# Turning h and the rows of x on VectorE, one block deeper, in a mixture-of-experts loop

## The reference

```python
x = hidden_states.reshape(-1, H)
logits = x @ gate_w
mult, sel = _sparse_mixer_routing(logits)
w = jnp.sum(mult[:, :, None] * (sel[:, :, None] == jnp.arange(E)[None, None, :]), axis=1)
h = jax.nn.silu(jnp.einsum('th,ehf->etf', x, w1)) * jnp.einsum('th,ehf->etf', x, w3)
out = jnp.einsum('etf,efh,te->th', h, w2, w)
```

## Time and profile before

| | |
|---|---|
| runs of the kernel before | 699.46, 698.66 and 1225.76 us; median 699.46 |
| profiled execution, first to last instruction | 697.2 us |
| busy in it: PE / DVE / ACT / POOL | 612.1 / 404.9 / 239.2 / 283.3 us |
| expert loop, from block 1's up to the last up | 327.36 to 663.45 us |
| end of the loop to the end of the span | 663.45 to 697.2 us |

### The profile page before, as it was taken

One profiled execution on the slowest core, in us unless ns is written; L12 is line 12 of the kernel. 1 busy time (PEld: TensorE's weight loads), 2 busy tenths in 40 slices (PEclk: granted clock), 3 DMA queues, 4 the chain that ended last, 5 costly groups with the idle time before them and its releaser, 6 DMA issues.

```text
span 697.2 us, 13581 instructions
## 1 busy us (share of the span) xinstructions
PE 612.1 (88%) x3780; PEld 482.2 (69%) x3781; DVE 404.9 (58%) x1214; ACT 239.2 (34%) x471; POOL 283.3 (41%) x198
## 2 busy tenths in 40 slices
PE   6999899798798875388999999999999999999940
PEld 2444469586366654367888888888888888888830
DVE  2566588766748879876544545445454454544524
ACT  3555540002876551224223242232422323321204
POOL 7000020012364456566516738167381373751112
...
GB/s 277 328 335 336 126 1 243 1 1 177 5 2 1 32 168 120 113 99 57 169 68 30 105 121 30 211 30 115 111 43 198 30 30 196 30 30 32 31 21 235
DMA packets 54003, 74.78 MB, mean 107 GB/s; under 512 B 13392, under 2 KB 50640, under 8 KB 52688
## 3 DMA queue, kind: packets, MB, share of 16 engines
...
...
## 4 chain that ended last, share of the span: by engine, by line
PE 68%; DVE 14%; POOL 5%; ACT 5%; DMA 4%; issue 3%; POOLq 0%; DVEq 0%; SPq 0%; ACTq 0%
PE bank L2197 26%; PE bank L2217 12%; PE bank L1769 7%; PE bank L1928 4%; PE bank L2207 4%; POOL experts_w L817 3%; DVE region L1259 2%; DVE region L1257 2%; DMA region<-slots 1%; PE bank L1819 1%; PE bank L1778 1%; PE bank L2152 1%; DVE small L1276 1%; PE bank L1785 1%; PE bank L2096 1%
## 5 line engine op out<-in xcount | busy, mean ns | idle before, releaser
L2197 PE MATMUL bank<-experts_w,experts_x 128*128 (+1 forms) x864 | 216.1, 399 | 3.6 <-POOL experts_w L817 2.3
L2197 PEld LDWEIGHTS bank<-experts_w,experts_x 128*128 128x128 f32 x864 | 157.0, 188 | 37.1 <-issue 4.4
L1701 DVE TENSOR_TENSOR region<-region,bank 128x512 f32<-128x512 f32 x72 | 49.5, 687 | 159.9 <-ACT region L1083 159.9
L1083 ACT ACTIVATE region<-bank 128x512 f32<-128x512 f32 x72 | 43.0, 597 | 238.5 <-PE bank L2197 238.5
L830 POOL DMA_INDIRECT total<-region,rid x36 | 55.8, 1549 | 165.2 <-DVE region L1715 105.8
L2217 PE MATMUL bank<-experts_w 128*128 (+1 forms) x864 | 120.9, 289 | 1.9 <-DVE experts_w L1705 1.9
L2217 PEld LDWEIGHTS bank<-experts_w 128*128 128x128 f32 x864 | 107.8, 191 | 2.2 <-issue 2.2
L817 POOL TENSOR_TENSOR experts_w<-wstage,experts_w 128x3072 f32 x12 | 83.6, 6964 | 0.5
L698 POOL TENSOR_TENSOR small<-small 128x4 f32<-128x4 f32 (+5 forms) x19 | 25.0, 1320 | 105.4 <-DVE small L1268 86.7
L1769 PE MATMUL bank<-xcol,region 128*128 128x512 f32 x128 | 59.0, 619 | 7.3 <-DMA xcol<-in_xT 5.7
L1155 DVE SCALAR_TENSOR_TENSOR region<-bank,convw,region 128x511 f32<-128x511 f32 (+2 forms) x48 | 35.9, 748 | 34.9 <-ACT region L873 33.0
...
...
## 6 DMA issues: line engine op xcount, KB each, us to landing
wstage<-in_w_exp SPq DMA_DIRECT2D x8, 3072.0 KB, 10.8
...
```

Source lines behind the costliest of these rows:

```text
L1083: act.activation(gsil[:, u], bank[2 * u][:, :], ACT.Silu).then_inc(sil_done, 1)
L1701: dve.tensor_tensor(hmid[:, u], gsil[:, u], bank[2 * u + 1][:, :], ALU.mult).then_inc(mid_done, 1)
L2197: mm = pe.matmul(bank[2 * u + m][:, :], (xTh, xTl)[a][:, s, k, :], moving(off, w, m * KD * F + k * F + u * HALF, HALF), start=(k == 0 and ...
```

## The change

- **Turns move from PE to DVE.** DVE's transpose turns blocks of 32x32. So h is first regrouped: `middle` writes `hmid` in four column groups, and SP's `regroup` copies each with a DMA from SBUF to SBUF into 32 partitions of `hgrp`, four DMAs a block of 128 pieces of 1 KB. DVE's `turn` (L1800) then turns 512 columns at once into the PSUM bank that PE wrote before. In the same way `load_rows` fetches x with four DMAs a block, in pieces of 32 values (128 B), and `rows` begins with a DVE transpose (L1720). The metadata gets its own small load, `load_meta`.
- **One block deeper.** In block g PE does up(g) and down(g-2). DVE does rows(g+1), row_meta(g-1), middle(g), turn(g-1), low_turned(g-1), weigh(g-2).
- **Weights in two parts.** SP loads the first 4096 columns (`load_up`) and the last 2048 (`load_down`) apart, in its own loop, behind the regrouping. ACT casts the first part (`high_up`), ahead of silu(g, 0). POOL takes its low part (`low_up`), and one block later splits the second part (`split_down`), behind a send.
- **The last block** is turned by PE (`last_turn`), into buffers of its own. `NB` grows from 42 to 48, so 8 pairs stand behind an `If` in place of 5 (two are taken). Each expert gets at least two blocks.

The diff, its core:

```diff
-NB = (2 * T + 2 * P + E * (P - 1)) // P + 1
-NB += NB % 2
+NB = 48
...
+        def rows_by_part(rows, a):
+            return rows[:, 0:D].rearrange("t (k a r) -> a t k r", a=NC, r=CH)[a]
...
+            def regroup(g, s):
+                if not isinstance(g, int) or g >= 2:
+                    sp.wait_ge(turned, 2 * g - 2)
+                    sp.sem_inc(sp_gate, 1)
+                sp.wait_ge(mid_done, 2 * g + 2)
+                for c in range(NC):
+                    sp.dma_start(hgrp[CH * c:CH * (c + 1), s].rearrange("p a q r -> p (a q r)"),
+                                 hmid[:, s, c].rearrange("p q r -> p (q r)")).then_inc(grouped[s], 16)
...
+            def load_ahead(g):
+                with sp.If(sp.value_load(tab_load[0:1, bass.ds(g - 1, 1)], min_val=0, max_val=1) > 0):
+                    event = event_of(g - 1)
+                    e = expert_of(event + 2)
+                    sp.wait_ge(w_low_up, event)
+                    load_up(e)
+                with sp.If(sp.value_load(tab_load[0:1, bass.ds(g - 2, 1)], min_val=0, max_val=1) > 0):
+                    event = event_of(g - 2)
+                    e = expert_of(event + 2)
+                    sp.wait_ge(w_ready, event + 2)
+                    load_down(e)
...
+            def pair(p):
+                regroup(2 * p - 1, 1)
+                load_ahead(2 * p - 1)
+                regroup(2 * p, 0)
+                load_ahead(2 * p)
...
+                    with pool.If(begins(g)):
+                        low_up(g)
+                    if isinstance(g, int) and g == 1:
+                        continue
+                    send_block(g - 2, s)
+                    with pool.If(begins(g - 1)):
+                        split_down(g - 1)
...
+            def load_rows(g, s):
+                rows = slots[bass.ds(slot_of(g), P), :]
+                act.wait_ge(xg_turned, g - 1)
+                for a in range(NC):
+                    act.dma_start(xq[CH * a:CH * (a + 1), s], rows_by_part(rows, a)).then_inc(xq_loaded[s], 16)
+
+            def load_meta(g, s):
+                slot = slot_of(g)
+                if not isinstance(g, int) or g >= 2:
+                    act.wait_ge(meta_done, g - 1)
+                act.dma_start(xm[:, s], slots[bass.ds(slot, P), D:ROW]).then_inc(xm_loaded[s], 16)
...
+            def high_up(g):
+                with act.If(act.value_load(tab_first[0:1, bass.ds(g, 1)], min_val=0, max_val=1) > 0):
+                    event = act.value_load(tab_event[0:1, bass.ds(g, 1)], min_val=1, max_val=E - 1)
+                    off = act.value_load(tab_noff[0:1, bass.ds(g, 1)], min_val=0, max_val=max(slot_at))
+                    act.wait_ge(up_done, 2 * g)
+                    act.wait_ge(w_up_loaded, 16 * event)
+                    act.sem_inc(act_gate, 1)
+                    act.copy(hi_of(off)[:, 0:ACT_PART], wstage[:, 0:ACT_PART]).then_inc(w_hi, 1)
...
+                    load_rows(g + 2, s)
+                    load_meta(g, s)
+                    if not start:
+                        high_up(g)
+                    silu(g, 0)
                     silu(g, 1)
-                    high_turned(g, 0)
-                    with act.If(act.value_load(tab_first[0:1, bass.ds(g, 1)], min_val=0, max_val=1) > 0):
-                        next_high(g)
-            def next_high(g):
-                event = act.value_load(tab_event[0:1, bass.ds(g, 1)], min_val=1, max_val=E - 1)
-                off = act.value_load(tab_noff[0:1, bass.ds(g, 1)], min_val=0, max_val=max(slot_at))
-                if not isinstance(g, int) or g:
-                    act.wait_ge(y_done, g)
-                act.wait_ge(w_loaded, 16 * event + 32)
-                act.sem_inc(act_gate, 1)
-                act.copy(hi_of(off)[:, 0:ACT_PART], wstage[:, 0:ACT_PART]).then_inc(w_hi, 1)
+                    for u in range(2):
+                        high_turned(g - 1, u)
+                    if start:
+                        high_up(g)
...
+                dve.wait_ge(xq_loaded[s], 32 * (g - s) + 64)
+                if isinstance(g, int) and g == 0:
+                    wait_drained(dve, ("f3", 1))
+                else:
+                    dve.wait_ge(xgT_done, g)
+                dve.transpose(bank[7][:, 0:D].rearrange("p (k r c) -> p c k r", k=KD, c=NC),
+                              xq[:, s].rearrange("p (c k r) -> p c k r", c=NC, k=KD)).then_inc(xg_turned, 1)
...
+            def middle(g, s, u):
                 dve.wait_ge(sil_done, 2 * g + (u + 1))
-                dve.tensor_tensor(hmid[:, u], gsil[:, u], bank[2 * u + 1][:, :], ALU.mult).then_inc(mid_done, 1)
-
-            def low_turned(g, u):
+                by_part = "p (c a r) -> p c a r"
+                dve.tensor_tensor(hmid[:, s, :, 4 * u:4 * u + 4].rearrange("p a c r -> p c a r"),
+                                  gsil[:, u].rearrange(by_part, a=NC, r=CH),
+                                  bank[2 * u + 1][:, :].rearrange(by_part, a=NC, r=CH), ALU.mult).then_inc(mid_done, 1)
+
+            def turn(g, s, u):
+                if u == 0:
+                    dve.wait_ge(grouped[s], 32 * (g - s) + 64)
+                if not isinstance(g, int) or g:
+                    dve.wait_ge(hTl_done, 2 * g + (u - 1))
+                dve.transpose(bank[4 + u][:, :].rearrange("p (c r a) -> p c a r", a=NC, r=CH),
+                              hgrp[:, s, :, 4 * u:4 * u + 4].rearrange("p a c r -> p c a r")).then_inc(turned, 1)
+
+            def low_turned(g, u, turned_in, high, low):
                 dve.wait_ge(hTh_done, 2 * g + (u + 1))
...
-                    row_meta(g + 1, 1 - s)
+                    row_meta(g - 1, 1 - s)
+                    for u in range(2):
+                        middle(g, s, u)
+                    for u in range(2):
+                        turn(g - 1, 1 - s, u)
+                    for u in range(2):
+                        low_turned(g - 1, u, bank[4 + u], hTh, hTl)
+                    if not isinstance(g, int) or g >= 2:
+                        weigh(g - 2, s)
...
+                    for u in range(2):
+                        up(g, s, u, off)
+                    if isinstance(g, int) and g == 1:
+                        continue
+                    off = offset_of(event_of(g - 2))
+                    for u in range(2):
+                        down(g - 2, u, off, hTh, hTl)
             pair(0)
+            pair(1)
             npair = pe.value_load(tab_n[0:1, 0:1], min_val=SURE, max_val=NB // 2)
-            with pe.Fori(0, SURE - 1) as it:
-                pair(it + 1)
+            with pe.Fori(0, SURE - 2) as it:
+                pair(it + 2)
             with pe.Fori(0, NB // 2 - SURE) as it:
                 with pe.If(npair - it > SURE):
                     pair(it + SURE)
...
+            off = offset_of(event_of(last - 1))
+            down(last - 1, 0, off, hTh, hTl)
+            for u in range(2):
+                last_turn(last, u)
+            down(last - 1, 1, off, hTh, hTl)
             off = offset_of(event_of(last))
-            turn(last, 1)
-            down(last, 0, off)
-            down(last, 1, off)
+            for u in range(2):
+                down(last, u, off, endTh, endTl)
```

266 lines of the change are left out of this document (133 added, 133 removed).

## The result

| | before | after |
|---|---|---|
| median of the runs | 700.64 us (4 runs) | 729.41 us (4 runs) |
| profiled execution | 697.2 us | 726.8 us |
| block 2's first silu to block 35's (33 blocks) | 319.0 us | 339.3 us |

One of the four executions of before took 1225.76 us and is left out of the ratio. The ratio after/before is 1.041 (95% interval 1.039 to 1.044): the change makes the kernel 4% slower, where 662 us, 5% faster, was forecast.

What follows compares the result with a forecast made beforehand. PE's work was taken to bound the expert loop: new loop 292.4 against 336.1 us (-43.7), end +6.4, so -37.3 and span 659.9; the median 2.3 us above gives 662 us. Summed bounds 651 to 680, stated range 650 to 690.

Steps and rivals of the forecast that it cites:

- Part 2: Ordinary block: DVE, ACT and transfers keep up with PE's 8.23 us; ACT's added issuing takes 3.6 us.
- Part 3: Six weight changes: ACT's cast ahead of silu(g, 0) makes PE wait about 1.5 us each, 9 us; bounds 0 to 18.
- The prediction's sign of being wrong: In the expert loop: the forecast is wrong if PE waits in every block, for DVE or through it.
- the two reasons that it named: For PE waiting in every block: DVE turns over 1.3 us, or a regrouping load that DVE waits for.
- Part 1: PE in the loop: loses 8 + 2 transposes, 1.32 us a block, so the floor falls from 9.55 to 8.23 us.
- Part 2, DVE: DVE in a block: turns add 1.67 us; it needs 6.7 of 8.23 us, with 1.5 us spare.
- The rival in which turning is slow: DVE's turns become the bound: 701 us at three times streaming time, 745 at four; chance of slower 0.15.
- the good case: DVE in the after profile: transposes of 0.6 to 0.75 us for 512 columns, waiting for silu once a block.
- Part 2, transfers: Small loads in a block: regrouped h has 6.5 us to land against a 2.1 us median; added bytes small.
- The rival of held-up transfers: Twelve weight loads delay the small transfers, stopping DVE: +12 to +24 us, 674 to 686; chance 0.14.
- The waits of PE for POOL: At new experts: the present waits, 2.3 us in all, go; margin 1 us.
- Part 4: Ends of the loop: start +1 us, behind two sets of row loads on ACT; end +6.4 us, bounds +4 to +9.

Runs made afterwards that it cites:

- G: Changed kernel with DVE turning each half of h twice, the second over the first; 779.54 us, ratio 1.112.
- B: Changed kernel with a block's rows of x fetched by one DMA of 1 KB pieces instead of four, x not regrouped; 691.12 us, ratio 0.981.
- C: Changed kernel with four row loads of 32 whole rows each instead of short pieces, x not regrouped; 701.45 us, ratio 0.997.
- D: Changed kernel with x turned by PE again and one row load a block, h still turned by DVE; 694.91 us, ratio 0.987.
- O: N plus one table read with its branch put back ahead of silu(g, 0) in every block; 708.83 us, ratio 1.008.
- J: Changed kernel with SP instead of ACT issuing the row loads, behind h's regrouping and a block earlier; 708.26 us, ratio 1.005.
- K: J plus the weight cast one block early, between silu(g-1, 1) and the high casts; 704.58 us, ratio 1.001.
- I: D with the weight cast moved one block early, between silu(g-1, 1) and the high casts; 680.87 us, ratio 0.964.
- N: Changed kernel with only the weight cast, and its table read, moved one block early, behind silu(g-1, 1); 689.90 us, ratio 0.981.
- M: Changed kernel with the loop's twelve expert-weight loads cut to 128 columns each; 736.62 us, ratio 1.049.
- L: K with the loop's twelve expert-weight loads cut to 128 columns each; 698.02 us, ratio 0.994.
- E: Changed kernel with row and metadata loads behind the silus and the weight cast last in ACT's block, behind the high casts; 753.20 us, ratio 1.076.
- F: D with ACT's order changed to silus, row and metadata loads, weight cast, high casts; 740.16 us, ratio 1.056.

## Why the prediction was wrong

**The sum, term by term**, in the profiled execution: forecast 659.9, measured 726.8, 66.9 us apart.

| part | forecast | measured | apart |
|---|---|---|---|
| to block 2's first silu | 336.9 | 345.55 | +8.6 |
| 27 ordinary blocks | 27 x 8.23 = 222.2 | 254.1 (9.41 each) | +31.9 |
| six blocks with a weight cast | 6 x 9.73 = 58.4 | 85.2 (14.2 each) | +26.8 |
| last silu(g, 0) to the end | 42.4 | 42.0 | -0.4 |

**The step that failed** is ACT's in Part 2: "5 x 0.42 + 3 x 0.5 = 3.6 us, from 3.0 to 6.7; then silu(g, 0) ... ends at 7.3, before DVE gets there." Measured, from the end of the high casts to the silu, it is 0.74 + 2.89 + 0.87 + 0.36 + 0.90 = 5.76 us. Two things were wrong with it. The price, in two terms of about the same size: an issue of 256 pieces costs 0.59 us and comes every 0.75 or so, for the 0.42 taken from a load of 128 pieces (four of them 2.89 us for 1.7); and the three stretches with a table read each took 0.74, 0.87 and 0.90 us, 2.5 together, for 3 x 0.5 = 1.5. The load's upper end was known to me and used ("0.5 or more"), but only in the bounds of Part 3, not in the ordinary block. And the form: I laid ACT's work out from a start at 3.0 and looked whether it ended in time once, but did not close the ring. ACT's start in a block hangs on DVE's turn, which hangs on ACT's silu. With 3.6 us for the issuing and the measured 1.1, 1.6 and 1.1 us of the rest, the sum round the ring is 7.4 us, 0.8 under the floor; with the measured 5.8 it is 9.5. So closing the ring alone would not have changed the forecast, but it would have shown that the margin was 0.8 us, less than the doubt in its prices. That the ring binds is what G shows, that the row loads' issuing is its largest part B, C and D, and that even one read in it counts in full O. The prediction's sign of being wrong, PE waiting in every block, came in most (42.5 us of waits for DVE's product, 20 times in the 33 blocks), but through ACT and for neither of the two reasons that it named.

**Part 1, PE's floor**, was mis-sized: 8.23 us forecast by taking the turns' pieces out of the earlier trace rows; where nothing else binds it is 8.47 (J and K). Turning costs PE 1.1 us a block, not 1.3. That alone is 8 us over 33 blocks, and no term of the range covered it.

**Part 2, DVE**, held: 0.70 us for a turn of h (0.61 in a row was forecast, 0.65 measured), 0.46 for x. The rival in which turning is slow did not come; DVE waits for silus, as forecast for the good case. The slow side was reached by another engine. The rule from the Trainium skill ("VectorE: DVE Perf Modes", "Rules for kernel authors"), that a 128x128 transpose belongs on TensorE where PSUM will do, names no reason that was at work here; for x the runs do not decide it. Turning it by PE costs PE 0.2 us a block and saves ACT three issues. I is faster than N (ratios 0.964 and 0.981, on different chips), but the 33 blocks differ by only 2.1 us (292.7 and 294.8); I's lead stands before block 2 (its silu at 343.1 and 352.7 us), where N had the lower clock named above, and N takes back 4.2 us of it at the end.

**Part 2, transfers**, held: in the changed kernel's loop DVE waited 10.3 us for rows (six times, at most 2.9), and M, which takes the weights' bytes away, leaves the loop as it was. The rival of held-up transfers came true in part only with more on SP's queue (7.2 us of K's 33 blocks, by L).

**Part 3, the weight changes**: 4.8 us each above an ordinary block for 1.5, since ACT had none of the slack that was counted on; it follows from the failed step, and from the cast's place between the issuing and the silus (O). The waits of PE for POOL went as forecast. That the cast must not come later was not seen at all; E and F show POOL's list, sends included, behind it.

**Part 4**: the end was right within 0.4 us when counted from the last block's first silu; the start was forecast 8.6 us too early. ACT's timeline shows block 1's silu right behind eight row loads, which take 6.66 us from 327.92 us on, where the forecast gave both sets 1 us; no run separates it.

**The clock**: 0.94 in the loop for 1.00. It fell behind PE's long waits, and in I and N, where those are gone, it is 1.00 from 400 us on. At one weight change the 24 matmuls behind the wait took 8.43 us, where the same 24 took 5.85 in the block before; how much of the longer block that makes was not measured by itself.
